# Graph layer with running maxima: three PSUM banks for the running rows, marks in two halves, table split tile by tile

## Chip, core and metric

One core of one Trainium2 chip. The metric is the device time of the kernel in microseconds; lower is better. Engines are named as in the profile: PE (TensorE), PEld (its weight loads), DVE (VectorE), ACT (ScalarE), POOL (GpSimd), SP (SyncE, which here only issues DMAs).

## What is computed

```python
# x (6250, 256) f32; src, dst (100000,) int32, sorted by dst; theta_w, phi_w (256, 256); theta_b, phi_b (256,)
x_src, x_dst = x[src], x[dst]
theta_x = (x_dst - x_src) @ theta_w.T + theta_b
phi_x = x_src @ phi_w.T + phi_b
e = jax.nn.relu(theta_x + phi_x)
out = jax.ops.segment_max(e, dst, num_segments=x.shape[0])
out = jnp.where(jnp.isfinite(out), out, 0.0)
return _layernorm(x + out, axis=-1)          # eps 1e-5
```

Since the edges are sorted by dst, the part that depends on src is b = x @ (phi - theta).T, and a node's result is relu(a + max of b over its edges), with a = x @ theta.T + biases.

## The kernel before, in words

The 100,000 edges lie as 128 partitions times 782 steps; partition p walks through its own 782 consecutive edges. At step k one row of b (256 f32) is needed for every partition, and one DVE instruction, the fold (L899), makes the running maximum: new = max(min(former, reset), row), where reset is a column with one number per partition that wipes the former value when a new node begins. The steps form 261 groups of three (GROUP). The kernel has these stages.

- **Table** (from the start to some 62 us). PE makes 49 tiles of b (L651), in seven chunks of seven; ACT copies each out of PSUM (L532). The tiles go to a table in HBM (L382, SP). At the same time each tile is split into three bf16 parts: ACT makes the first (L534) and second (L522), DVE the remainders `rest` (L832) and the third part (L824), in units of four and three tiles, so as instructions over 1024 and 768 elements. DVE's have two tensor inputs, both in SBUF. Meanwhile POOL gathers 51 x rows by indirect DMA (`early`, L464); ahead of the units DVE prepares `reset` and other columns (L785 to L818).
- **Fold loop** (to some 939 us). Most rows of b come by indirect DMA from the table, issued by POOL (L478), one per step, 679 of them, into a ring of 18 (`rows`). Before a group POOL waits until the fold that read the slot 18 gathers earlier is done (L476). The other steps, always the first of a group, get their rows in other ways: 51 from x rows that PE turns (L689) and converts (L697), with copies by ACT at L573 and L569; 40 from products of one-hot matrices (L851, DVE) with the bf16 parts in SBUF (L673, PE), in ten batches of 49, copied by ACT at L599 and L606; 12 from DMAs of one row each (L396 by SP, L562 by ACT). HOT_AT gives 2.12 one-hots to each group; six of them may be ahead of PE.
- In a group, the first two folds write `acc` in PSUM (two rows of a bank, the two banks in turn), and the third writes `hist` in SBUF, a ring of 18 rows. So the first fold of a group reads the former row from `hist`, the other two from `acc`. ACT then copies the two rows of `acc` to `hist` (L581), DVE waits for the copy of group g - 2 before it folds group g, and SP writes the group's three rows to HBM (L429, `runmax`). In the last eight groups (from LATE on) all folds write `hist`, and after each fold DVE also keeps the row at which each partition's last complete node ends (look_at, L871, `late_max`).
- **Marks.** In every fourth group DVE makes three small masks (L910 to L916), PE spreads the dst numbers of one node tile over the partitions into `ps_d` (L707, L708; two banks), and ACT, one group later, counts with one Sign activation over 782 columns how many edges lie up to a node (L588, L590). At EDGES_AT (L918) DVE makes row numbers of the counts.
- **a tiles** (in the fold loop's last part): L734 on PE, L950 on DVE.
- **End.** After the last fold: PE turns the last maxima, DVE scans over the partitions (L956), joins `late_max`, a gathered row `fix` and the carry (L961, L964), POOL scatters the result (L495) and gathers 49 tiles of maxima (L504), and DVE and ACT add, apply relu and normalise (L996 to L1016, L615).

The order on each engine is the order in the text of its loop over g, with semaphores between engines. Nothing else plans it. Behind an ACT copy in group g stand, in this order, its row loads, the Sign, and the copies of the products; ahead of it stand L569 and L573.

Of the kernel before, what the change touches and what calls it, by code (L numbers as in the profile page):

```python
# [39 lines left out]
def build(nc, x, xt, src_first, src_direct, src_act, src, src_t, dst, theta_t, phi_t, theta_b, phi_b, out):  # L40
# [6 lines left out]
    HALF = 2 * D  # L47
# [4 lines left out]
    assert HALF < STEPS <= 2 * HALF and NT * P <= 1 << 13 and 2 * CHUNK <= SLOTS  # L52
# [65 lines left out]
    LATE_STEPS = STEPS - KEPT  # L118
    assert ENDS_AT < LATE and CLEAR_AT < LATE
# [38 lines left out]
    with ExitStack() as ctx:  # L158
# [6 lines left out]
        def sem(name):  # L165
# [48 lines left out]
        in_row = sb("in_row", [P, NT])  # L214
        edges = sb("edges", [P, NT + 1])
# [43 lines left out]
        acc = ps("acc", [P, 4, D])  # L259
# [3 lines left out]
        ps_d = ps("ps_d", [P, 4, D])  # L263
        dst_rows = ps_d[:].rearrange("p j d -> p (j d)")
        rows_of_nodes = dst_rows[:, 4 * D - NT:4 * D]
        assert STEPS <= 4 * D - NT
        b_psum = [acc[:, 0, :], acc[:, 2, :], ps_t[:, 0, :], ps_a[0][:, 0, :], ps_a[1][:, 0, :], ps_a[2][:, 0, :],
                  ps_d[:, 0, :]]
# [30 lines left out]
        s_copied = sem("groups_copied")  # L299
# [50 lines left out]
        def _(sp):  # L350
# [64 lines left out]
            for g in range(NG):  # L415
# [39 lines left out]
        def _(pool):  # L455
# [15 lines left out]
            pool.wait_ge(s_rest, UNITS)  # L471
# [39 lines left out]
        def _(act):  # L511
# [6 lines left out]
            def second_part(u):  # L518
                tiles, _ = unit(u)
                n = tiles.stop - tiles.start  # L520
                act.wait_ge(s_rest, u + 1)
                nc.scalar.copy(split[:, 1, tiles, :], rest[:, u % 2, 0:n, :]).then_inc(s_split2, 1)  # L522

            for u in range(UNITS):
                c, part = divmod(u, 2)
                tiles, places = unit(u)
                if c >= 2:
                    act.wait_ge(s_bout[c % 2], 16 * (c // 2))
                    act.wait_ge(s_rest, u - 3)
# [35 lines left out]
            for g in range(NG):  # L565
# [19 lines left out]
                if g in SIGN_AT:  # L585
                    t = SIGN_AT[g]
                    act.wait_ge(s_dstrow, t + 1)
                    nc.scalar.activation(dst_rows[:, 0:STEPS], dst_rows[:, 0:STEPS], ACT.Sign, bias=part_up[:, 0:1],  # L588
                                         scale=-1.0, accum_out=in_row[:, t:t + 1]).then_inc(s_inrow, 1)
# [51 lines left out]
        def _(pe):  # L641
# [18 lines left out]
            def select(b, t):  # L660
                i = b * NT + t
                if i == 0:
                    pe.wait_ge(s_split1, UNITS)
                    pe.wait_ge(s_split2, UNITS)
                    pe.wait_ge(s_split3, UNITS)
# [16 lines left out]
            for g in range(NG):  # L682
# [69 lines left out]
        def _(dve):  # L752
# [67 lines left out]
            def third_part(u):  # L820
                tiles, _ = unit(u)
                n = tiles.stop - tiles.start
                dve.wait_ge(s_split2, u + 1)
                nc.vector.scalar_tensor_tensor(split[:, 2, tiles, :], split[:, 1, tiles, :], -1.0, rest[:, u % 2, 0:n, :],  # L824
                                               ALU.mult, ALU.add).then_inc(s_split3, 1)

            for u in range(UNITS):
                tiles, places = unit(u)
                dve.wait_ge(s_split1, u + 1)
                if u >= 2:  # L830
                    dve.wait_ge(s_split3, u - 1)
                nc.vector.scalar_tensor_tensor(rest[:, u % 2, 0:tiles.stop - tiles.start, :], split[:, 0, tiles, :], -1.0,  # L832
                                               rows[:, places, :], ALU.mult, ALU.add).then_inc(s_rest, 1)
# [10 lines left out]
            def mark_sources(b, t):  # L844
# [4 lines left out]
                elif i == 0:  # L849
                    dve.wait_ge(s_split3, UNITS)  # L850
# [15 lines left out]
            def look_at(k, row):  # L866
                i = k - KEPT
                dve.wait_ge(s_fold, k + 1)
                if i:
                    dve.wait_ge(s_late, i)  # L870
                nc.vector.scalar_tensor_tensor(late_max[:], row, is_fix[:, i:i + 1], late_max[:], ALU.min,  # L871
                                               ALU.max).then_inc(s_late, 1)

            former, before = none[:], None
            for g in range(NG):
                n, slot, at = STOP[g] - START[g], g % HELD * GROUP, g % 2 * 2
# [8 lines left out]
                if 2 <= g < LATE:  # L885
                    dve.wait_ge(s_copied, g - 1)
                for s in range(n):
# [5 lines left out]
                    new = acc[:, at + s, :] if s < n - 1 and g < LATE else hist[:, slot + s, :]  # L893
                    if s == (n - 1 if g < LATE else 0) and g >= HELD:
                        dve.wait_ge(s_hout[g % HELD], 16 * (g // HELD))
# [169 lines left out]
```

## Time and profile before

| | |
|---|---|
| median of 3 runs | 1024.68 us (1023.37 to 1027.84) |
| profiled execution | 1024.78 us, span 1022.9 us |
| PE, DVE, ACT, POOL busy | 825.9, 692.4, 338.2, 762.6 us |
| mean granted TensorE clock | 0.929 |
| folds end, scatter of the fixed rows starts | 939.4, 943.2 us |

Busy time leaves out register, branch, semaphore and DMA-issuing instructions, save POOL's indirect DMAs, where the time is that of making their descriptors. A row of a view begins with line, engine, operation, output <- inputs, shapes and count.

### The profile page before, as it was taken

Reading aid. Unit: us, or ns where it says so; the run is one execution under the profiler, and the core shown is the slowest. Engines: PE = TensorE matmul, PEld = TensorE weight load, DVE = VectorE, ACT = ScalarE, POOL = GpSimd, SP = SyncE. Lnnn points to the kernel's source line nnn. Section 1 sums busy time; section 2 is a strip of 40 time slices with the busy share of each in tenths; the row PEclk is TensorE's granted clock in tenths of the full one; section 3 lists DMA queues with packets and bytes.
Section 4 is the critical chain, followed back from the end, with each engine's and each line's share of the span. In section 5 each row is a group of like instructions: output and inputs, shape, how many; then the busy total and the mean of one; then the engine's idle time right before and its main releaser. Section 6 shows DMA issues by size and latency. Waiting matters only on the chain. (4 is left out here: it accounts for less than half of the span.)

```text
span 1022.9 us, 17761 instructions
## 1 busy us (share of the span) xinstructions
PE 825.9 (81%) x3806; PEld 436.7 (43%) x3875; DVE 692.4 (68%) x1733; ACT 338.2 (33%) x701; POOL 762.6 (75%) x788
## 2 busy tenths in 40 slices
PE   5977899999999999999999999999998846560000
PEld 5833444445454545555445455445443324340000
DVE  6645666776676767667767676767665646565798
ACT  4831233333332333242333242333231121110466
POOL 7777777777777777777777777777777777775773
PEclk9979999999999999999999999999999969985555
DMA  8955767777777777867777877777776789975465
GB/s 281 379 180 181 224 223 242 230 254 236 257 235 246 243 229 252 267 221 257 239 242 241 262 226 251 240 250 237 257 226 219 235 279 308 284 241 164 122 203 176
DMA packets 117745, 243.93 MB, mean 238 GB/s; under 512 B 20241, under 2 KB 58982, under 8 KB 117638
## 3 DMA queue, kind: packets, MB, share of 16 engines
q1 hardware_dynamic: 78244, 138.69, 37.7%
q0 software_dynamic: 37488, 102.39, 35.1%
q10 hardware_dynamic: 1906, 1.72, 0.7%
q8 instruction: 31, 0.51, 0.2%
q14 instruction: 76, 0.62, 0.2%
HBM read 127.30 MB, written 115.45 MB: 237 GB/s over the span
## 5 line engine op out<-in xcount | busy, mean ns | idle before, releaser
L478 POOL DMA_INDIRECT rows<-b_table,idx x679 | 654.6, 964 | 207.0 <-issue 173.8
L673 PE MATMUL ps_a<-work,shared 128*128 128x512 bf16 x2876 | 657.1, 381 | 36.9 <-DVE work L851 33.1
L673 PEld LDWEIGHTS ps_a<-work,shared 128*128 128x128 bf16 x2940 | 282.3, 98 | 375.5 <-DVE work L851 37.2
L581 ACT COPY hist<-acc 128x512 f32<-128x512 f32 x253 | 148.7, 588 | 362.2 <-DVE hist L899 358.3
L899 DVE SCALAR_TENSOR_TENSOR acc<-hist,reset,rows 128x256 f32<-128x256 f32 x149 | 73.5, 494 | 198.2 <-issue 151.4
L851 DVE TENSOR_SCALAR work<-batch,node 128x512 bf16<-128x512 int16 x490 | 160.5, 371 | 6.1 <-PE ps_a L673 6.1
L899 DVE SCALAR_TENSOR_TENSOR acc<-acc,reset,rows 128x256 f32<-128x256 f32 x253 | 124.7, 493 | 40.7 <-DMA rows<-b_table,idx 26.8
L899 DVE SCALAR_TENSOR_TENSOR hist<-acc,reset,rows 128x256 f32<-128x256 f32 x253 | 122.3, 483 | 26.2 <-DVE acc L899 0.5
L734 PE MATMUL ps_a<-theta_sb,shared 128*128 128x256 f32 x196 | 54.4, 429 | 39.2 <-DVE shared L950 30.6
L464 POOL DMA_INDIRECT early<-in_x,idx_first x51 | 56.2, 1103 | 17.1 <-issue 14.9
L734 PEld LDWEIGHTS ps_a<-theta_sb,shared 128*128 128x128 f32 x196 | 39.9, 213 | 53.8 <-issue 48.2
L588 ACT ACTIVATE ps_d<-ps_d,part_up 128x782 f32<-128x782 f32 x49 | 43.6, 889 | 53.3 <-issue 50.3
L504 POOL DMA_INDIRECT rows<-runmax,end_row x49 | 48.4, 987 | 16.3 <-issue 14.6
L697 PE MATMUL ps_rows<-diff_sb,conv_t 128*128 128x256 f32 x204 | 52.4, 379 | 0.1
L697 PEld LDWEIGHTS ps_rows<-diff_sb,conv_t 128*128 128x128 f32 x204 | 38.4, 190 | 9.4
L573 ACT COPY conv_t<-ps_rows 128x256 f32<-128x256 f32 x51 | 19.1, 374 | 67.1 <-PE ps_rows L689 49.4
L569 ACT COPY early<-ps_rows 128x256 f32<-128x256 f32 x51 | 19.1, 375 | 63.8 <-PE ps_rows L697 61.4
L615 ACT ACTIVATE hist<-hist,shift,rstd 128x256 f32<-128x256 f32 x49 | 25.4, 586 | 0.0
L899 DVE SCALAR_TENSOR_TENSOR acc<-hist,reset,early 128x256 f32<-128x256 f32 x51 | 24.6, 482 | 0.2 <-issue 0.2
L651 PE MATMUL acc<-diff_sb,hist 128*128 128x256 f32 x56 | 15.0, 415 | 11.3 <-DMA hist<-in_xt 11.3
L832 DVE SCALAR_TENSOR_TENSOR work<-shared,rows 128x1024 f32<-128x1024 bf16 (+1 forms) x14 | 15.2, 1090 | 12.5 <-ACT shared L534 12.5
L707 PE MATMUL ps_d<-from_tile,row_of 128*128 128x270 bf16 (+1 forms) x93 | 23.1, 326 | 0.3
(133 smaller groups left out, 483.9 us busy)
## 6 DMA issues: line engine op xcount, KB each, us to landing
runmax<-hist SPq DMA_DIRECT2D x260, 384.0 KB
direct<-b_table SPq DMA_DIRECT2D x896, 1.0 KB
rows<-b_table,idx POOLq DMA_INDIRECT x679, 3.5
b_table<-rows SPq DMA_DIRECT2D x7, 896.0 KB, 7.6
shared<-in_xt SPq DMA_DIRECT2D x49, 128.0 KB, 4.4
early<-in_x SPq DMA_DIRECT2D x12, 512.0 KB
out<-hist SPq DMA_DIRECT2D x11, 512.0 KB, 3.3
late_max<-b_table ACTq DMA_DIRECT2D x256, 1.0 KB
```

The lines of the kernel that those rows point to most:

```text
L464: pool.indirect_dma_start(out=early[:, e, :], out_offset=None, in_=x, in_offset=bass.IndirectOffsetOnAxis(ap=idx_first[:, e:e + 1], axis=0 ...
L478: pool.indirect_dma_start(out=rows[:, PLACE[k], :], out_offset=None, in_=b_table, in_offset=bass.IndirectOffsetOnAxis(ap=idx[:, k:k + 1], ...
L504: pool.indirect_dma_start(out=rows[:, slot + i, :], out_offset=None, in_=runmax, in_offset=bass.IndirectOffsetOnAxis(ap=end_row[:, t + i:t ...
L581: nc.scalar.copy(hist[:, slot:slot + n - 1, :], acc[:, at:at + n - 1, :]).then_inc(s_copied, 1)
L588: nc.scalar.activation(dst_rows[:, 0:STEPS], dst_rows[:, 0:STEPS], ACT.Sign, bias=part_up[:, 0:1], scale=-1.0, accum_out=in_row[:, t:t + 1 ...
L615: nc.scalar.activation(hist[:, i, :], hist[:, i, :], ACT.Identity, scale=rstd[:, i:i + 1], bias=shift[:, i:i + 1]).then_inc(s_norm, 1)
L673: mm = pe.matmul(ps_a[banks(b)[k]][:].rearrange("p j d -> p (j d)"), split[:, part, t, k * P:(k + 1) * P], hot[:, i % HOT, :], start=(t == ...
L697: mm = pe.matmul(ps_b[:, 0, :], conv_t[:, k, :], diff_sb[:, k, :], start=(k == 0), stop=(k == KC - 1))
L707: pe.matmul(dst_rows[:, at:at + n], row_of[:], from_tile[:, at:at + n], start=True, stop=True)
L734: mm = pe.matmul(ps_a[t % 2][:, 0, :], xt_late[:, t % (2 * CHUNK), k, :], theta_sb[:, k, :], start=(k == 0), stop=(k == KC - 1))
L851: nc.vector.tensor_scalar(hot[:, i % HOT, :], short_sources[:, b % 2, :], node[:, t:t + 1], None, ALU.is_equal).then_inc(s_hot, 1)
L899: nc.vector.scalar_tensor_tensor(new, former, reset[:, k:k + 1], row_at(k), ALU.min, ALU.max).then_inc(s_fold, 1)
```

## The change

All folds but the last four now write `acc`, which is a ring of six rows in three banks. ACT copies pairs of rows to `hist`, pair (k, k+1) when fold k + 2 is done; fold k, for even k, waits for the copy of the pair that is six steps back. Copies go on to the end of the loop. look_at reads `acc` and comes after every second fold; for the last four steps it keeps its maximum in a PSUM row (`late_acc`), joined with one more instruction at the end. `ps_d` has one bank, so a node tile's marks are spread and counted in two halves of 391 columns, two groups apart. The remainders and third parts of the table are made tile by tile.

```diff
-    HALF = 2 * D
+    HALF = STEPS // 2
...
-    SPREAD_AT = {5 + 4 * t: t for t in range(NT)}
-    SIGN_AT = {6 + 4 * t: t for t in range(NT)}
-    EDGES_AT, ENDS_AT = 4 + 4 * NT, 8 + 4 * NT
+    SPREAD_AT = {5 + 4 * t + 2 * half: (t, half) for t in range(NT) for half in range(2)}
+    SIGN_AT = {6 + 4 * t + 2 * half: (t, half) for t in range(NT) for half in range(2)}
+    EDGES_AT, ENDS_AT = 7 + 4 * NT, 11 + 4 * NT
...
+    ROUND = 6
+    COPIED = STEPS - 4
+    PAIRS_AT = [range(max(0, STOP[g - 1] - 1) // 2 if g else 0, max(0, min(STOP[g], COPIED + 1) - 1) // 2) for g in range(NG)]
...
-        acc = ps("acc", [P, 4, D])
+        acc = ps("acc", [P, ROUND, D])
...
-        ps_d = ps("ps_d", [P, 4, D])
+        ps_d = ps("ps_d", [P, 2, D])
...
-                if g < LATE:
-                    sp.wait_ge(s_copied, g + 1)
-                else:
+                sp.wait_ge(s_copied, (min(STOP[g], COPIED) + 1) // 2)
+                if STOP[g] > COPIED:
                     sp.wait_ge(s_fold, STOP[g])
...
-                if g == LATE:
-                    break
-                n, slot, at = STOP[g] - START[g], g % HELD * GROUP, g % 2 * 2
-                act.wait_ge(s_fold, STOP[g])
-                if g >= HELD:
-                    act.wait_ge(s_hout[g % HELD], 16 * (g // HELD))
-                nc.scalar.copy(hist[:, slot:slot + n - 1, :], acc[:, at:at + n - 1, :]).then_inc(s_copied, 1)
+                for pair in PAIRS_AT[g]:
+                    k = 2 * pair
+                    act.wait_ge(s_fold, k + 3)
+                    for before in written((k, k + 1)):
+                        act.wait_ge(s_hout[before % HELD], 16 * (before // HELD + 1))
+                    nc.scalar.copy(hist[:, k % SLOTS:k % SLOTS + 2, :],
+                                   acc[:, k % ROUND:k % ROUND + 2, :]).then_inc(s_copied, 1)
...
-                    nc.scalar.activation(dst_rows[:, 0:STEPS], dst_rows[:, 0:STEPS], ACT.Sign, bias=part_up[:, 0:1],
-                                         scale=-1.0, accum_out=in_row[:, t:t + 1]).then_inc(s_inrow, 1)
+                    nc.scalar.activation(dst_rows[:, 0:HALF], dst_rows[:, 0:HALF], ACT.Sign, bias=part_up[:, 0:1],
+                                         scale=-1.0, accum_out=in_half[:, half, t:t + 1]).then_inc(s_inrow, 1)
...
-                    t = SPREAD_AT[g]
-                    pe.wait_ge(s_from, t + 1)
-                    pe.wait_ge(s_rowof, t + 1)
-                    if t:
-                        pe.wait_ge(s_inrow, t)
-                    for at, n in ((0, HALF), (HALF, STEPS - HALF)):
-                        pe.matmul(dst_rows[:, at:at + n], row_of[:], from_tile[:, at:at + n], start=True, stop=True)
-                    pe.matmul(rows_of_nodes[:, t:t + 1], row_of[:], p_col[:], start=True,
+                    t, half = SPREAD_AT[g]
+                    if not half:
+                        pe.wait_ge(s_from, t + 1)
+                        pe.wait_ge(s_rowof, t + 1)
+                    if t or half:
+                        pe.wait_ge(s_inrow, 2 * t + half)
+                    if not half:
+                        pe.matmul(rows_of_nodes[:, t:t + 1], row_of[:], p_col[:], start=True, stop=True)
+                    pe.matmul(dst_rows[:, 0:HALF], row_of[:], from_tile[:, half * HALF:(half + 1) * HALF], start=True,
                               stop=True).then_inc(s_dstrow, 1)
...
-                nc.vector.scalar_tensor_tensor(split[:, 2, tiles, :], split[:, 1, tiles, :], -1.0, rest[:, u % 2, 0:n, :],
-                                               ALU.mult, ALU.add).then_inc(s_split3, 1)
+                for t in range(tiles.start, tiles.stop):
+                    nc.vector.scalar_tensor_tensor(split[:, 2, t, :], split[:, 1, t, :], -1.0,
+                                                   rest[:, u % 2, t - tiles.start, :], ALU.mult,
+                                                   ALU.add).then_inc(s_split3, 1)
...
-                if 2 <= g < LATE:
-                    dve.wait_ge(s_copied, g - 1)
...
-                    new = acc[:, at + s, :] if s < n - 1 and g < LATE else hist[:, slot + s, :]
+                    new = acc[:, k % ROUND, :] if k < COPIED else hist[:, k % SLOTS, :]
+                    if k < COPIED and k % 2 == 0 and k >= ROUND:
+                        dve.wait_ge(s_copied, (k - ROUND) // 2 + 1)
...
-                    if k > KEPT:
-                        look_at(k - 1, hist[:, before, :])
-                    before = slot + s
+                    if KEPT < k < COPIED and k % 2:
+                        for i in range(k - 1, k + 1):
+                            look_at(i, acc[:, i % ROUND, :], late_max[:], False)
+                    elif k == KEPT:
+                        look_at(k, new, late_max[:], False)
+                    elif k > COPIED:
+                        look_at(k - 1, hist[:, (k - 1) % SLOTS, :], late_acc, k - 1 == COPIED)
...
+            nc.vector.scalar_tensor_tensor(fix[:], late_acc, 1.0, fix[:], ALU.mult, ALU.max).then_inc(s_best, 1)
+            dve.wait_ge(s_best, 1)
             nc.vector.tensor_tensor(late_max[:], late_max[:], fix[:], ALU.max).then_inc(s_best, 1)
```

## Rows read from the trace of the kernel before

**Rows 1.** The page's chain that ended last, and the longest waits of the span.

```profile
DVE 4%; POOL 2%; issue 2%; DMA 1%; ACT 0%; PE 0%; POOLq 0%; DVEq 0%
...
POOL rows L478 <- issue: 173.8, 570, 0.3
...
DVE acc L899 <- ACT hist L581: 29.1, 28, 4.1
```

**Rows 2.** POOL by line, one line's instructions: duration ns min/median/max.

```profile
L464 POOL DMA_INDIRECT early<-in_x,idx_first x51: 942/946/1917, 3.8 to 74.3; - x51
...
L478 POOL DMA_INDIRECT rows<-b_table,idx x679: 942/946/2067, 75.6 to 934.8; - x170
```

**Rows 3.** POOL's groups by stretch (0:75, 75:912, 912:937): busy us, mean ns, idle.

```profile
L464 POOL DMA_INDIRECT early<-in_x,idx_first x51 | 56.2, 1103 | 17.1 <-issue 14.9 <-DMA idx_first<-in_src_first 1.9 <-DVE work L832 0.3
...
L478 POOL DMA_INDIRECT rows<-b_table,idx x661 | 635.6, 962 | 201.5 <-issue 169.8 <-DVE acc L899 22.2 <-DVE hist L899 9.4
...
L478 POOL DMA_INDIRECT rows<-b_table,idx x19 | 20.0, 1051 | 5.8 <-issue 4.3 <-DVE hist L899 0.9 <-DMA runmax<-hist 0.6
```

**Rows 4.** Timeline of POOL, then of DVE, 45 to 61 us: start us, us.

```profile
46.53 1.80 POOL L464 DMA_INDIRECT early<-in_x,idx_first  x1 [0.30 <-issue]
...
46.29 1.22 DVE L824 SCALAR_TENSOR_TENSOR shared<-shared,work 128x1024 bf16<-128x1024 bf16 x1
...
59.46 2.09 DVE L824 SCALAR_TENSOR_TENSOR shared<-shared,work 128x1024 bf16<-128x1024 bf16 x2
```

**Rows 5.** Timeline of POOL, then of DVE, 453 to 457 us.

```profile
453.69 1.11 POOL L478 DMA_INDIRECT rows<-b_table,idx  x1 [0.30 <-issue]
455.11 1.08 POOL L478 DMA_INDIRECT rows<-b_table,idx  x1 [0.30 <-DVE hist L899]
...
453.50 0.49 DVE L899 SCALAR_TENSOR_TENSOR acc<-hist,reset,rows 128x256 f32<-128x256 f32 x1 [2.25 <-ACT hist L581]
...
454.63 0.48 DVE L899 SCALAR_TENSOR_TENSOR hist<-acc,reset,rows 128x256 f32<-128x256 f32 x1
455.03 0.61 DVE L851 TENSOR_SCALAR work<-batch,node 128x512 bf16<-128x512 int16 x2
```

**Rows 6.** Timeline of all engines, 583 to 592 us.

```profile
585.11 3.37 ACTq L562 DMA_DIRECT2D late_max<-b_table  x3
...
586.71 0.48 DVE L899 SCALAR_TENSOR_TENSOR hist<-acc,reset,rows 128x256 f32<-128x256 f32 x1
586.86 0.95 POOL L478 DMA_INDIRECT rows<-b_table,idx  x1 [0.30 <-issue]
```

**Rows 7.** Timeline of the fold loop's last microseconds.

```profile
934.79 2.07 POOL L478 DMA_INDIRECT rows<-b_table,idx  x1 [0.30 <-issue]
935.56 0.48 DVE L871 SCALAR_TENSOR_TENSOR late_max<-hist,is_fix,late_max 128x256 f32<-128x256 f32 x1
...
940.95 0.40 DVE L961 TENSOR_TENSOR late_max<-late_max,fix 128x256 f32<-128x256 f32 x1
...
941.88 0.42 DVE L964 TENSOR_TENSOR late_max<-late_max,ps_rows 128x256 f32<-128x256 f32 x1 [0.53 <-PE ps_rows L747]
```

**Rows 8.** DVE's, ACT's costliest groups of the page: busy us, mean ns, idle before.

```profile
L581 ACT COPY hist<-acc 128x512 f32<-128x512 f32 x253 | 148.7, 588 | 362.2 <-DVE hist L899 358.3
L899 DVE SCALAR_TENSOR_TENSOR acc<-hist,reset,rows 128x256 f32<-128x256 f32 x149 | 73.5, 494 | 198.2 <-issue 151.4
L851 DVE TENSOR_SCALAR work<-batch,node 128x512 bf16<-128x512 int16 x490 | 160.5, 371 | 6.1 <-PE ps_a L673 6.1
...
L588 ACT ACTIVATE ps_d<-ps_d,part_up 128x782 f32<-128x782 f32 x49 | 43.6, 889 | 53.3 <-issue 50.3
```

**Rows 9.** Windows: us, then busy (x) of PE, PEld, DVE, ACT, POOL; clock.

```profile
382.00:482.00 100.00, 99.47 (x479) 50.61 (x488) 71.64 (x186) 33.55 (x70) 75.89 (x80) 1.00 0.76 249
...
682.00:782.00 100.00, 93.08 (x430) 44.65 (x437) 67.24 (x180) 28.40 (x55) 75.93 (x80) 0.98 0.74 238
782.00:832.00 50.00, 35.77 (x162) 16.07 (x163) 27.27 (x68) 9.76 (x17) 37.91 (x40) 0.91 0.72 232
```

**Rows 10.** L950, one tile of 128x256 alone.

```profile
L950 DVE SCALAR_TENSOR_TENSOR shared<-ps_a,bias x49: 408/414/425, 837.6 to 921.6; 128x256 f32<-128x256 f32 x49
```

More of the change, by code:

```diff
@@ L51, in build @@
     assert NT % CHUNK == 0 and CHUNKS % 2 == 1 and D % P == 0 and sum(PARTS) == CHUNK
-    assert HALF < STEPS <= 2 * HALF and NT * P <= 1 << 13 and 2 * CHUNK <= SLOTS
+    assert STEPS == 2 * HALF and NT * P <= 1 << 13 and 2 * CHUNK <= SLOTS
     START = list(range(0, STEPS, GROUP))
@@ L118, in build, with written @@
     LATE_STEPS = STEPS - KEPT
+    ROUND = 6
+    COPIED = STEPS - 4
+    PAIRS_AT = [range(max(0, STOP[g - 1] - 1) // 2 if g else 0, max(0, min(STOP[g], COPIED + 1) - 1) // 2) for g in range(NG)]
+    assert COPIED % 2 == 0 and PAIRS_AT[-1].stop == COPIED // 2 and SLOTS % 2 == 0
+    def written(rows):
+        return {(k - SLOTS) // GROUP for k in rows if k >= SLOTS}
     assert ENDS_AT < LATE and CLEAR_AT < LATE
@@ L214, in build @@
         in_row = sb("in_row", [P, NT])
+        in_half = sb("in_half", [P, 2, NT])
         edges = sb("edges", [P, NT + 1])
@@ L262, in build @@
         ps_a = [ps(f"ps_a{i}", [P, 2, D]) for i in range(3)]
-        ps_d = ps("ps_d", [P, 4, D])
+        ps_d = ps("ps_d", [P, 2, D])
         dst_rows = ps_d[:].rearrange("p j d -> p (j d)")
[L265 to L268, printed above, removed]
+        rows_of_nodes = dst_rows[:, 2 * D - NT:2 * D]
+        late_acc = ps_d[:, 0, :]
+        assert HALF <= 2 * D - NT
+        b_psum = [acc[:, 0, :], acc[:, 2, :], acc[:, 4, :], ps_t[:, 0, :], ps_a[0][:, 0, :], ps_a[1][:, 0, :],
+                  ps_a[2][:, 0, :]]
         assert len(b_psum) == CHUNK
@@ L470, in _ @@
             pool.wait_ge(s_bout[1], 16 * (CHUNKS // 2))
-            pool.wait_ge(s_rest, UNITS)
+            pool.wait_ge(s_rest, NT)
             for g in range(NG):
@@ L520, in second_part @@
                 n = tiles.stop - tiles.start
-                act.wait_ge(s_rest, u + 1)
+                act.wait_ge(s_rest, tiles.stop)
                 nc.scalar.copy(split[:, 1, tiles, :], rest[:, u % 2, 0:n, :]).then_inc(s_split2, 1)
@@ L830, in _ @@
                 if u >= 2:
-                    dve.wait_ge(s_split3, u - 1)
-                nc.vector.scalar_tensor_tensor(rest[:, u % 2, 0:tiles.stop - tiles.start, :], split[:, 0, tiles, :], -1.0,
-                                               rows[:, places, :], ALU.mult, ALU.add).then_inc(s_rest, 1)
+                    dve.wait_ge(s_split3, unit(u - 2)[0].stop)
+                for t in range(tiles.start, tiles.stop):
+                    i = t - tiles.start
+                    nc.vector.scalar_tensor_tensor(rest[:, u % 2, i, :], split[:, 0, t, :], -1.0,
+                                                   rows[:, places.start + i, :], ALU.mult, ALU.add).then_inc(s_rest, 1)
                 if u:
@@ L864, in row_at, with look_at @@
                 return rows[:, PLACE[k], :] if k in PLACE else early[:, EARLY_OF[k], :]
-            def look_at(k, row):
+            looked = [0]
+            def look_at(k, row, best, first):
                 i = k - KEPT
                 dve.wait_ge(s_fold, k + 1)
-                if i:
-                    dve.wait_ge(s_late, i)
-                nc.vector.scalar_tensor_tensor(late_max[:], row, is_fix[:, i:i + 1], late_max[:], ALU.min,
+                if looked[0]:
+                    dve.wait_ge(s_late, looked[0])
+                looked[0] += 1
+                nc.vector.scalar_tensor_tensor(best, row, is_fix[:, i:i + 1], late_max[:] if first else best, ALU.min,
                                                ALU.max).then_inc(s_late, 1)
-            former, before = none[:], None
+            former = none[:]
             for g in range(NG):
-                n, slot, at = STOP[g] - START[g], g % HELD * GROUP, g % 2 * 2
+                n = STOP[g] - START[g]
                 if START[g] in EARLY_OF:
@@ L892, in _ @@
                         dve.wait_ge(s_got[g % LANDED], ARRIVED[g])
-                    new = acc[:, at + s, :] if s < n - 1 and g < LATE else hist[:, slot + s, :]
-                    if s == (n - 1 if g < LATE else 0) and g >= HELD:
-                        dve.wait_ge(s_hout[g % HELD], 16 * (g // HELD))
+                    new = acc[:, k % ROUND, :] if k < COPIED else hist[:, k % SLOTS, :]
+                    if k < COPIED and k % 2 == 0 and k >= ROUND:
+                        dve.wait_ge(s_copied, (k - ROUND) // 2 + 1)
+                    if k >= COPIED:
+                        for earlier in written((k,)):
+                            dve.wait_ge(s_hout[earlier % HELD], 16 * (earlier // HELD + 1))
                     if k:
@@ L918, in _ @@
                 if g == EDGES_AT:
-                    dve.wait_ge(s_inrow, NT)
+                    dve.wait_ge(s_inrow, 2 * NT)
+                    then(nc.vector.tensor_tensor(in_row[:], in_half[:, 0, :], in_half[:, 1, :], ALU.add))
                     then(nc.vector.tensor_scalar(in_row[:], in_row[:], 0.5, 0.5 * STEPS, ALU.mult, ALU.add))
@@ L951, in _ @@
                                                    ALU.add).then_inc(s_aev, 1)
-            look_at(STEPS - 1, former)
+            look_at(STEPS - 1, former, late_acc, False)
             dve.wait_ge(s_lastt, 1)
```

17 lines of the change are left out of this document (8 added, 9 removed).

## The prediction

> **What bounds the kernel now.** First the chain of waits: it holds little more than the last tenth of the span, and its long pieces are POOL's indirect DMAs and, behind them, DVE's work on the output tiles [rows 1]. So the question is what POOL waited for earlier, and the list of waits answers it: of 679 gathers 570 stand behind "issue", never over 0.3 us at a time [rows 1]. By line [rows 2], an undisturbed gather takes 0.946 us (the median), the x rows' and the table's alike, and the gap is always 0.30. POOL therefore runs one gather each 1.25 us from 3.8 us to 937 us and waits for nobody, neither for the table nor for a free slot. DVE, with 198 us idle before the first fold of its groups, waits for POOL [rows 8]. Nothing that other engines do in that stretch counts unless it makes a gather longer, or makes POOL wait at all.
>
> Some gathers are longer. By stretch [rows 3], the 51 early ones took 56.2 us, 8.0 over 51 x 0.946; the next 661 took 635.6, 10.3 over; the last 19 took 20.0, 2.0 over. That is 20.3 us of POOL's time and nearly all that any edit to the other engines can return before 937 us.
>
> What stretches them shows when POOL's timeline is laid beside DVE's. In [rows 4] a gather begins at 46.53 and takes 1.80, 0.85 too long. A remainder instruction of DVE with two inputs in SBUF runs from 46.29 to 47.51. In [rows 5] the gather of 453.69 took 1.11, and a fold that reads `hist` and `rows` runs from 453.50 to 453.99. The sum is the same in both: the excess is the end of DVE's instruction less POOL's start less 0.135 us (0.98 - 0.135 = 0.85; 0.30 - 0.135 = 0.165), if DVE's began at least 0.08 before POOL's. The next gather in [rows 5], from 455.11, took 1.08: the first of two one-hot instructions (L851) began 0.08 before it. I went through all starts between 75.5 and 912 us in this way. Of 101 gathers that began with a fold reading `hist` under way 42 were stretched, 4.7 us in all (first at 93.09, last at 908.68), and L851 accounts for about 5.2. Of the 171 that began under a fold with its former row in PSUM none was stretched, as at 586.86 in [rows 6].
>
> **The folds in PSUM.** After the change a fold has one SBUF input. This removes the 4.7 us of the first folds, with an occasional second hold (4.9 with starts where both kinds overlap). What of L851's 5.2? Some twenty of its hits are a consequence of a fold hit: POOL, released at the fold's end, starts the next gather 0.49 - 0.135 + 1.25 = 1.605 us after the fold's start, and the first L851 starts 1.53 after it (455.03 - 453.50), always 0.08 ahead [rows 5]. These go with their cause. Against that, L851 moves: three folds through PSUM at 0.59 spacing, the distance that a fold reading the one before it in `acc` shows, end about 0.1 us later than now, and other groups come to lie badly. Without any lock, 480 L851 meet a window of 0.135 us (0.08 to 0.215 before a gather) in 1.25, with 0.067 us each: 52 x 0.067 = 3.5 us. The bounds are 0 and about 8 (each group's second L851 in the window that now holds the most first folds). I take 3.6 left of 10.3: **6.7 us saved** (2.3 to 10.3).
>
> Weighed against this is the Trainium skill, SBUF — State Buffer, Who interferes with whom. It says that a DVE instruction with two SBUF inputs contends with a GpSimd instruction that reads SBUF, the loser waiting to the end; but also that such an instruction takes only the pair's read interface, while making descriptors needs the write interface (marked as inferred). By its second half this change would return nothing and the time would stay at 1025. This trace sides with the first half: 1.80 against 0.946 with only such an instruction beside it [rows 4].
>
> **The last eight groups.** There folds and look_at both read two SBUF tensors, 46 instructions of 0.48, and the last gather took 2.07 [rows 7], through the ends of four of them in a row. After the change only the folds of steps 779 to 781 have two SBUF inputs. Of 2.0 us I take **1.8 saved** (1.0 to 2.0), the greater part of it in the last gather, whose landing releases the last fold.
>
> **The table tile by tile.** Of the 8.0 us over, 1.05 lie in the preparation ahead of the units, which stays; 6.9 come from L832 and L824, 28 instructions of 0.95 to 1.23. They become 98 of some 0.42 (a tile's instruction took 0.414 [rows 10]), and two that follow each other start about 0.33 apart. A gather that begins under one now waits at most 0.42 - 0.08 - 0.135 = 0.2 us, with a mean near 0.065, and about 26 begin under one: 1.7 us. **5.2 us saved**. Could POOL miss the gap between two instructions that overlap by 0.08, and wait out all four tiles? In [rows 4] it did not: two L824 follow each other from 59.46, and the gather of 59.70 ended with the first. The 2.07 in [rows 7] says that it can. The bounds are then 7 saved, and 1 lost (four times 0.33 plus 0.09 is 1.41 against 1.23). DVE's work grows by some 28 x 0.15 = 4 us, but it waits for ACT's casts there, and the table is in HBM by 62.6 while POOL comes to it at 75 (now 70): covered, cost 0. If that cover of 7 us were gone the loss would be one for one.
>
> **More copies, smaller slack.** 389 pair copies replace 253 at 0.588 [rows 8]: ACT has 80 us more, and 49 more Signs of half width (0.889 for 782 columns; half of them between 0.45 and 0.889, I take 0.55, plus the accumulator read of 0.19) add 49 x 0.6 = 29. ACT goes from 338 to 447 us of 1011, no bound. But in even groups the pair of rows 3g - 2 and 3g - 1 stands behind L569 or L573, which wait for PE's previous group, and is wanted by the group's fifth fold from its start; before, the seventh. PE has no idle time to hide (99.5 of 100 us busy in mid-loop [rows 9]), so DVE will wait more often for ACT: 29.1 us in 28 waits now [rows 1], I take 60 to 80. Folds in PSUM take 0.25 us more a group, 63 us. Both come out of DVE's idle time (198 us before first folds alone [rows 8]). POOL notices only when DVE is more than 18 x 1.25 - 3.5 (landing) - 4 = 15 us behind. None of it counts: **0**. SP writes a group about one group later, at 16 of the 20 us that the `hist` ring allows; 0 as well. POOL's queue is not touched.
>
> **The end.** The two last look_at go through PSUM one after the other (0.1 later), and the added join of 0.42 stands before L961 and L964. L961 ended at 941.35 and L964 began at 941.88 [rows 7], so of 0.47 about 0.53 is free: **0.2 us added** (0.1 to 0.6). From the scatter at 943.2 to the end nothing changes.
>
> **Sum.** 1024.8 (profiled execution: 1022.9 of span and 1.9 around it; the median of the runs is the same within 0.1) - 5.2 - 6.7 - 1.8 + 0.2 = **1011.3 us**. All bounds together give 1024.8 - 7 - 10.3 - 2 + 0.1 = 1005.6 and 1024.8 + 1 - 2.3 - 1 + 0.6 = 1023.1, but they would have to fall together.
>
> **Rivals.** (a) The contention moves: L851 comes to lie on POOL's starts (6 to 8 us instead of 3.6), or POOL waits out chains of tiles in the table. For it: this kernel's phases are locked, so hits are not random; against it: most chains seen let POOL in. Half of the table's gain and 3 us of the loop's are gone: 1011.3 + 2.6 + 3.2 = 1017. (b) Nothing moves: what stretched the gathers was not the second SBUF input but something that goes with it. For it only the page's sentence above; against it 0 of 171. Time 1025. (c) Slower: PE waits for the Sign. Today a tile's Sign has three groups; now each half has one. Behind the group's last fold ACT makes a copy (0.59), three row loads (1.3, but 3.37 where row numbers are loaded [rows 6]), Sign and read (0.74), 2.6 to 4.7 us, while PE has 2.12 x 6 matmuls of 100/479 us, 2.7 us, before it asks. PE's own spare time before the products end is at least 6.9 + 14.2 us [rows 9], then DVE may lag 15 us. So it decides from (21 + 15)/98 = 0.37 us for each of 98 waits; at 0.6 us it costs 59 - 36 = 23: 1034. Against it: where PE lags behind DVE, as it does in most of the loop, the Sign is done when PE comes.
>
> **How the numbers follow.** Forecast 0.74, (a) 0.13, (b) 0.05, (c) 0.08. A difference under 0.5% (5.1 us) can't be told from none. Faster: the first and nearly all of (a), 0.86; same 0.06; slower 0.08. The forecast's own bounds reach from 1006.5 to 1016; with (a) the range ends at 1019, and (b), (c) and the far ends, under 0.2, are left out.
>
> **What would show it.** Right: POOL's early group near 50 us busy for 51 (from 56.2), the 679 gathers near 646 (from 654.6), still with gaps of 0.3 only; no stretched gather under a fold; the last gather below 1.2 us. DVE's wait for ACT above 29 and without effect. Wrong: gathers stretched under folds with a PSUM input, a wait of POOL for a fold over 1 us, PE idle before the spreads (L707, L708), or a scatter that starts more than 4.5 us after the last fold.

## The result and the profile after

The changed kernel takes 1012.7 us in the median (1012.2 to 1012.9), the kernel before 1025.2: ratio 0.9875, 95% interval 0.9853 to 0.9898. The forecast was 1011.3, range 1006.5 to 1019. The profiled execution has a span of 1011.1 us, 11.8 shorter.

The page of the changed kernel, its costliest groups (busy us, mean ns, idle before):

```profile
L488 POOL DMA_INDIRECT rows<-b_table,idx x679 | 646.1, 952 | 207.0 <-issue 181.4
...
L590 ACT COPY hist<-acc 128x512 f32<-128x512 f32 x389 | 221.5, 592 | 224.9 <-DVE acc L917 222.8
...
L598 ACT ACTIVATE ps_d<-ps_d,part_up 128x391 f32<-128x391 f32 x98 | 55.3, 564 | 70.8 <-issue 67.5
L474 POOL DMA_INDIRECT early<-in_x,idx_first x51 | 52.1, 1021 | 17.2 <-issue 15.2
```

POOL's idle time is what it was, 207.0 us, in gaps of 0.3; its gathers are shorter. The same groups by stretch, POOL alone, 71 to 900 us and 900 to 925 us, answer to [rows 3]:

```profile
L488 POOL DMA_INDIRECT rows<-b_table,idx x660 | 628.2, 952 | 201.2 <-issue 176.5 <-DVE acc L917 24.7
...
L488 POOL DMA_INDIRECT rows<-b_table,idx x20 | 18.9, 946 | 6.1 <-issue 4.9 <-DVE acc L917 0.6 <-DMA runmax<-hist 0.6
```

Over 0.946 us each, the early gathers are now 3.9 us too long (8.0 before), the loop's 3.8 (10.3), the last twenty 0 (2.0). The three savings are 4.1, 6.5 and 2.0, together 12.6; the forecast had 5.2, 6.7 and 1.8.

Folds no longer stretch a gather. A start counts here when it lies at least 0.08 us after the start of the DVE instruction and more than 0.135 us before its end. Before, 42 of 48 such starts under a fold that reads `hist` were stretched by over 0.04 us, and none of 98 under a fold that reads `acc`; now all folds of the loop read `acc` and none of 161 starts was stretched. The one-hots (L865) still stretch theirs, 44 of 45 by over 0.02 us, though they have one tensor input; by what they hold POOL no run here separates.

By line (duration ns min/median/max), the longest gather of the loop fell from 2067 to 1107 ns [rows 2]:

```profile
L488 POOL DMA_INDIRECT rows<-b_table,idx x679: 942/946/1107, 71.5 to 923.4; - x170
```

In the table stage, timeline of POOL and then of DVE, 45 to 61 us, to be read against [rows 4]:

```profile
45.61 1.11 POOL L474 DMA_INDIRECT early<-in_x,idx_first  x1 [0.30 <-issue]
47.02 1.04 POOL L474 DMA_INDIRECT early<-in_x,idx_first  x1 [0.30 <-issue]
48.37 0.94 POOL L474 DMA_INDIRECT early<-in_x,idx_first  x1 [0.30 <-issue]
...
45.48 1.43 DVE L846 SCALAR_TENSOR_TENSOR work<-shared,rows 128x256 f32<-128x256 bf16 x4 [1.24 <-ACT shared L544]
46.83 1.09 DVE L835 SCALAR_TENSOR_TENSOR shared<-shared,work 128x256 bf16<-128x256 bf16 x3
```

The gather of 45.61 began under four tile instructions in a row that last until 46.91, and took 1.11. Held to 46.91 it would have taken 2.11 (1.30 - 0.135 + 0.946): POOL got in after one of them. Of 27 gathers that began under such instructions 19 were stretched, by 2.3 us in all; the other eight began within 0.02 us of the start of the next one in the row.

The end, timeline of all engines, answers to [rows 7]:

```profile
923.43 0.95 POOL L488 DMA_INDIRECT rows<-b_table,idx  x1 [0.30 <-issue]
...
926.84 0.48 DVE L917 SCALAR_TENSOR_TENSOR hist<-hist,reset,rows 128x256 f32<-128x256 f32 x1
927.23 1.07 DVE L888 SCALAR_TENSOR_TENSOR ps_d<-hist,is_fix,ps_d 128x256 f32<-128x256 f32 x2
...
928.86 0.40 DVE L984 SCALAR_TENSOR_TENSOR fix<-ps_d,fix 128x256 f32<-128x256 f32 x1
...
929.79 0.42 DVE L989 TENSOR_TENSOR late_max<-late_max,ps_rows 128x256 f32<-128x256 f32 x1
931.24 1.03 POOL L505 DMA_INDIRECT runmax<-late_max,fix_row  x1 [5.54 <-issue]
```

POOL's last gather now ends at 924.38 and not 936.86, 12.5 us earlier, the last fold starts 12.1 us earlier (926.84 for 938.92), the scatter 12.0 (931.24 for 943.21), and the end comes 11.8 earlier. The 0.4 lost between the first two is a wait that took the place of one: before, the last fold waited for its row (2.1 us behind the gather); now the row is there, and the fold follows DVE's own folds and look_at without a gap.

The engines that were thought to come under pressure (waits of the whole span):

```profile
DVE acc L917 <- ACT hist L590: 14.2, 16, 3.1
...
DVE from_tile L937 <- PE ps_d L719: 11.1, 16, 1.6
...
PE ps_d L719 <- ACT ps_d L598: 1.7, 5, 0.5
```

DVE waits for ACT's copies half as long as before (29.1 us), not longer, and PE almost never waits for a Sign (2.2 us in 6 waits with those of L718). A new wait stands ahead of the masks: DVE may not overwrite `from_tile` until PE has spread its second half. It is within DVE's idle time.

For the experiments one thing must be known: beside ten of the twelve runs the kernel before itself took 1377 to 1393 us in the median, not 1025, and POOL was not the bound. Such runs are marked **P**. In their ten traces ACT waits 298 to 551 us and DVE 160 to 260 us for what the profile calls "remote", a semaphore raised by nothing that it recorded, up to 18.7 us at a time; the four traces at 1011 to 1041 us have no such wait. The mean granted TensorE clock is 0.81 to 0.84 in them, against 0.92 to 0.93. What is cause and what consequence there is open. P times are compared only with the kernel before that was timed beside them; the length of a single gather can be read in them as elsewhere, since the median one takes 0.946 to 0.949 us there too. Only the last two, e8_sbuf_five and e6c_nine, met a kernel before at 1027 us.

### The profile page after: what moved, and what is told of

Same layout as the page of the kernel before. It is cut to its first block, busy times and chain, and to the rows that moved or that the text cites. A ratio compares the mean times of both kernels' runs of the same rounds, so it can differ in the third digit from the quotient of the medians.

```text
span 1011.1 us, 18234 instructions
## 1 busy us (share of the span) xinstructions
PE 832.0 (82%) x3875; PEld 438.2 (43%) x3875; DVE 696.6 (69%) x1805; ACT 421.4 (42%) x935; POOL 750.0 (74%) x788
## 4 chain that ended last, share of the span: by engine, by line
PE 34%; POOL 21%; DMA 18%; issue 11%; DVE 11%; ACT 2%; ACTq 2%; SPq 0%; DVEq 0%; POOLq 0%
PE ps_a L683 28%; POOL rows L488 19%; DMA rows<-b_table,idx 14%; DVE acc L917 5%; DMA b_table<-rows 2%; PE ps_rows L707 2%; POOL rows L514 2%; DVE work L865 1%; DVE shared L1024 1%; PE acc L661 1%; ACTq L569 1%; DVE shared L1021 1%; DVE stats L1038 1%; PE ps_d L719 1%; ACT hist L590 1%
## 5 line engine op out<-in xcount | busy, mean ns | idle before, releaser
L488 POOL DMA_INDIRECT rows<-b_table,idx x679 | 646.1, 952 | 207.0 <-issue 181.4
L917 DVE SCALAR_TENSOR_TENSOR acc<-acc,reset,rows 128x256 f32<-128x256 f32 x674 | 331.5, 492 | 249.7 <-DMA rows<-b_table,idx 197.6
L590 ACT COPY hist<-acc 128x512 f32<-128x512 f32 x389 | 221.5, 592 | 224.9 <-DVE acc L917 222.8
L865 DVE TENSOR_SCALAR work<-batch,node 128x512 bf16<-128x512 int16 x490 | 160.6, 371 | 5.3 <-PE ps_a L683 5.3
L598 ACT ACTIVATE ps_d<-ps_d,part_up 128x391 f32<-128x391 f32 x98 | 55.3, 564 | 70.8 <-issue 67.5
L719 PE MATMUL ps_d<-from_tile,row_of 128*128 128x391 bf16 x98 | 32.2, 329 | 1.7 <-ACT ps_d L598 1.7
L661 PE MATMUL acc<-diff_sb,hist 128*128 128x256 f32 x84 | 22.2, 420 | 12.6 <-DMA hist<-in_xt 12.6
L937 DVE TENSOR_SCALAR from_tile<-short_dst 128x782 bf16<-128x782 int16 x49 | 19.6, 401 | 12.4 <-PE ps_d L719 11.1
L846 DVE SCALAR_TENSOR_TENSOR work<-shared,rows 128x256 f32<-128x256 bf16 x49 | 18.0, 426 | 11.1 <-ACT shared L544 10.5
L917 DVE SCALAR_TENSOR_TENSOR acc<-acc,reset,early 128x256 f32<-128x256 f32 x51 | 24.6, 481 | 0.0
L661 PEld LDWEIGHTS acc<-diff_sb,hist 128*128 128x128 f32 x84 | 17.3, 210 | 16.2 <-issue 10.6
```

What stands on the lines that cost most here:

```text
L488: pool.indirect_dma_start(out=rows[:, PLACE[k], :], out_offset=None, in_=b_table, in_offset=bass.IndirectOffsetOnAxis(ap=idx[:, k:k + 1], ...
L590: nc.scalar.copy(hist[:, k % SLOTS:k % SLOTS + 2, :], acc[:, k % ROUND:k % ROUND + 2, :]).then_inc(s_copied, 1)
L598: nc.scalar.activation(dst_rows[:, 0:HALF], dst_rows[:, 0:HALF], ACT.Sign, bias=part_up[:, 0:1], scale=-1.0, accum_out=in_half[:, half, t: ...
L661: mm = pe.matmul(b_psum[j], xt_sb[:, h * CHUNK + j, k, :], diff_sb[:, k, :], start=(k == 0), stop=(k == KC - 1))
L719: pe.matmul(dst_rows[:, 0:HALF], row_of[:], from_tile[:, half * HALF:(half + 1) * HALF], start=True, stop=True).then_inc(s_dstrow, 1)
L865: nc.vector.tensor_scalar(hot[:, i % HOT, :], short_sources[:, b % 2, :], node[:, t:t + 1], None, ALU.is_equal).then_inc(s_hot, 1)
```

## The experiments

Theory P (a name that has nothing to do with the mark): POOL never waits, so a gather costs 1.25 us, and each start under a DVE instruction with two SBUF inputs, or under a one-hot, adds what is left of that instruction. The rivals are in the expectations.

**e1_table (P): only the table tile by tile.** The kernel before with

```diff
-                nc.vector.scalar_tensor_tensor(rest[:, u % 2, 0:tiles.stop - tiles.start, :], split[:, 0, tiles, :], -1.0,
-                                               rows[:, places, :], ALU.mult, ALU.add).then_inc(s_rest, 1)
+                for t in range(tiles.start, tiles.stop):
+                    ...
```

> The kernel before with only the table's remainders and third parts made tile by tile. Theory P (POOL never waits, and only stretched gathers cost time): of the 7.0 us by which the early gathers exceed 0.946 us each behind the preparation about 4.7 go, as in the changed kernel (2.3 left), the fold loop stays as it was: 1025.2 - 4.7 = 1020.5. Rival T (the table is not what counts, all of the gain is the ring's): 1025 +- 1. Rival C (POOL waits out chains of overlapping tile instructions): 1025 to 1027, with gathers of over 1.5 us between 17 and 62 us.

1387.5 us, ratio 1.020 (0.992 to 1.049): it can't be told from no change. POOL's 51 early gathers took 50.0 us, but DVE stood idle for 28.8 us of that stage, and ACT and PE for 8 to 11 us at a time, so only four gathers began under a tile instruction, and that is no measure of them either. For the time it is inconclusive. Its loop, whose folds are those of the kernel before, shows both kinds of fold in one trace: 41 of 44 starts under one that reads `hist` were stretched, by 3.6 us, and none of 105 under one that reads `acc`.

**e2_ring and e2b_ring (P): only the ring, the pair copies and the halves.** The changed kernel with

```diff
-                for t in range(tiles.start, tiles.stop):
-                    i = t - tiles.start
-                    nc.vector.scalar_tensor_tensor(rest[:, u % 2, i, :], split[:, 0, t, :], -1.0,
+                nc.vector.scalar_tensor_tensor(rest[:, u % 2, 0:tiles.stop - tiles.start, :], split[:, 0, tiles, :], -1.0,
...
```

> The changed kernel with the table again in units of four and three tiles: ring of six rows, pair copies and marks in halves alone. Theory P: 6.4 us of the loop's stretched gathers and 1.9 of the last eight groups' go, 0.2 comes at the end: 1025.2 - 8.1 = 1017.1. Rival T: all of the gain, 1012.7. If the two parts share their gain (the phases of POOL and DVE fall otherwise), the sum of both savings differs from 12.5 us by more than 2.

> The same kernel as e2_ring, again, for its time where the kernel before takes 1025 and not 1377 to 1392 us. Ring, pair copies and halves alone, the table in units of four and three tiles. Theory P: 1025.2 - 8.1 = 1017.1. Rival T (all of the gain is the ring's): 1012.7. If the kernel before again takes near 1380 us, POOL isn't the bound there, and theory P expects no gain: DVE, ACT and PE wait longer for each other, and the ring's shorter slack makes it 0 to 3% slower, as in e2_ring.

1391.1 and 1404.0 us, ratios 1.024 (1.010 to 1.038) and 1.016 (1.006 to 1.025): slower, by 1 to 2%. The first ratio goes by the two shortest of seven times of the kernel before (1349.9 and 1362.9); against the median of all seven, 1377.3, it would be 1.010. The gathers are those of the changed kernel (679 in 646.4 us, none of 165 starts under a fold stretched in e2, none of 161 in e2b), so the ring shortens them, and it returns nothing where they do not set the pace. How the gain of 12.5 splits in time was not measured at 1025, and against rival T, that all of it is the ring's, speaks only the split above, which is that of POOL's durations.

**d1_two_sbuf and d2_one_psum (P): one more DVE instruction a group.** In the changed kernel, between folds and one-hots; d1 as shown, d2 with `former` for `theta_sb[:, 0, :]` (`s_spare` is a new semaphore):

```diff
+                if g < LATE:
+                    k = STOP[g]
+                    dve.wait_ge(s_fold, k)
+                    if k % 2 == 0 and k >= ROUND:
+                        dve.wait_ge(s_copied, (k - ROUND) // 2 + 1)
+                    nc.vector.scalar_tensor_tensor(acc[:, k % ROUND, :], theta_sb[:, 0, :], 1.0, bias[:], ALU.min,
+                                                   ALU.max).then_inc(s_spare, 1)
+                    dve.wait_ge(s_spare, g + 1)
```

> The changed kernel with one more DVE instruction in each of 253 groups, between the folds and the one-hots: 128x256 f32 of two inputs in SBUF (theta_sb, bias), written to the acc slot that the next fold overwrites; its value is not used. Theory P: a hold of 0.49 us catches a start of POOL with a window of 0.27 in 1.25 us, 55 times with 0.135 us: 1012.7 + 7.4 = 1020 (1016 to 1027, since the starts are not random), and gathers stretched under it. Rival W (what stretches gathers is not the second SBUF input: a DVE instruction's write, or DVE's load as such): the same time as d2_one_psum.

> The same added instruction, but its first input is the row just folded, in PSUM, so that only bias is read from SBUF. Theory P: no gather is stretched under it; DVE is busy 253 x 0.49 = 124 us more, out of some 250 us of waiting; one-hots come about 0.5 us later against POOL, so their hits move: 1012.7 + 0 (-2 to +3). Rival W: as slow as d1_two_sbuf. Rival L (DVE's load now decides, PE starved): above 1018 in both.

1393.8 and 1393.6 us: in time no difference, and none could show, as POOL waited for folds 336 and 334 us; the 1020 and 1012.7 of the forecasts were not tested. The gathers tell them apart. Timeline of POOL and DVE, d1:

```profile
380.86 1.10 POOL L489 DMA_INDIRECT rows<-b_table,idx  x1 [0.30 <-issue]
...
380.71 0.43 DVE L934 SCALAR_TENSOR_TENSOR acc<-theta_sb,bias 128x256 f32<-128x256 f32 x1
```

and d2:

```profile
372.95 0.94 POOL L489 DMA_INDIRECT rows<-b_table,idx  x1 [2.62 <-DVE acc L918]
...
372.71 0.43 DVE L934 SCALAR_TENSOR_TENSOR acc<-acc,bias 128x256 f32<-128x256 f32 x1
```

Both instructions take 0.43 us, write the same slot and stand in the same place. Of 56 starts under d1's, counted as above, 53 were stretched by over 0.03 us, by 5.5 us together (0.28 - 0.135 = 0.145 forecast for the one shown, 1.10 - 0.946 = 0.154 measured). Of 42 under d2's none was. Rival W falls: for this instruction it is the second SBUF input, neither the write nor DVE's load.

**e3_all_sbuf (P) and e8_sbuf_five: the suspected cost made larger.** The kernel before with all folds written to SBUF and no copies by ACT, as in the diff; e8 has also `DIRECT_GROUPS = (46, 89, 130, 174, 217)` and `ROWS_A_GROUP = 3`.

```diff
-                nc.scalar.copy(hist[:, slot:slot + n - 1, :], acc[:, at:at + n - 1, :]).then_inc(s_copied, 1)
...
-                    new = acc[:, at + s, :] if s < n - 1 and g < LATE else hist[:, slot + s, :]
+                    new = hist[:, slot + s, :]
```

> The kernel before with all three folds of every group written to SBUF (hist), as its last eight groups do, and without ACT's copies out of PSUM. Theory P: all folds hold two SBUF inputs, 0.40 us apart, so in most groups one of POOL's starts falls under a fold; 253 x 0.86 x about 0.1 us is 22 us in place of 4.7: 1025.2 + 17 = 1042 (1030 to 1055), POOL's gathers longer in the mean and still no wait of POOL. Rival A (the load of ACT and the longer folds through PSUM set the time; 148 us of copies and 0.2 us a group are gone): 1015 to 1025.

> e3_all_sbuf (the kernel before, all folds written to SBUF, no copies by ACT) with e7_five's five steps of rows loaded by SP: the two edits that saved time where the kernel before takes near 1385. Theory S (the pace is set there by instructions that SP and ACT issue, each for itself): the savings add, 1385 - 28 - 47 = 1310 (1295 to 1330). Rival O (both remove the same wait): 1335 to 1365. Where the kernel before takes 1025, theory P expects it slower than before: two gathers and more stretched ones, 1035 to 1055.

e3 took 1363.3 us, ratio 0.978 (0.972 to 0.983): faster, though the gathers grew to 672.7 us. That is the side of rival A (ACT's 148 us of copies gone), but the waits for these copies and the order of the writes to HBM went with them, and which of it counted was not separated. e8 met a kernel before of 1026.6 and took 1043.4, ratio 1.0165 (1.0148 to 1.0182), inside the 1035 to 1055 of theory P; theory S and rival O were not tested, as the kernel before was not at 1385. Its gathers, by line, with POOL's only named wait still "issue" at up to 0.3 us:

```profile
L475 POOL DMA_INDIRECT rows<-b_table,idx x681 | 669.9, 984 | 207.7 <-issue 176.9
...
L461 POOL DMA_INDIRECT early<-in_x,idx_first x51 | 58.1, 1139 | 17.2 <-issue 15.2
```

Against [rows 3] and the page of the kernel before that is 15.3 + 1.9 us more busy and 0.8 more in gaps, 18.0, for 16.8 us of time (18.4 between the two profiled spans); two of the gathers are additional (2.5). Of 144 starts under a fold of the loop, counted as above, 132 were stretched by over 0.02 us, by 21.0 us (4.7 before). One of them, POOL and DVE:

```profile
338.64 1.21 POOL L475 DMA_INDIRECT rows<-b_table,idx  x1 [0.31 <-issue]
...
338.54 1.00 DVE L889 SCALAR_TENSOR_TENSOR hist<-hist,reset,rows 128x256 f32<-128x256 f32 x2
```

The rest of the first fold (0.38 - 0.135 = 0.25) went by and no more: the second, 0.08 inside the first's end, did not hold POOL. In this kernel ACT has less to do than in the kernel before (198.8 us busy for 338.2), SP issues 256 row loads less and DVE is as busy (693.2 us for 692.4), and it is the slowest of the four at 1012 to 1043: the gathers decide.

**e6_nine, e6b_nine (P) and e6c_nine: two gathers less.** The changed kernel with

```diff
-DIRECT_GROUPS = (35, 69, 98, 130, 162, 194, 226)
+DIRECT_GROUPS = (30, 54, 81, 105, 131, 157, 182, 207, 234)
-ROWS_A_GROUP = 4
+ROWS_A_GROUP = 5
```

> The changed kernel with nine steps in place of seven whose rows SP loads one by one (five rows a group in place of four), so POOL has 677 gathers in place of 679. Theory P: two gathers of 1.25 us less, 1012.7 - 2.5 = 1010.2 (1009 to 1011.5). Rival Q (SP's queue or DMA traffic is near its limit; DVE waits for direct rows or for hist): 1012.7 or more, with waits of DVE for those rows.

> The same kernel as e6_nine, again, since in that comparison the kernel before took 1391 us and not 1025, and its time can't be set beside the forecast. Nine steps in place of seven have their rows loaded one by one by SP, so POOL has two gathers less. Theory P: 1012.7 - 2 x 1.25 = 1010.2 (1009 to 1011.5) where the kernel before takes 1025. Rival Q (SP's queue is near its limit): 1012.7 or more.

> The nine-step kernel (677 gathers by POOL in place of 679) once more, now that the kernel before takes 1026 us again. Theory P: two gathers of 1.25 us less than the changed kernel, 1.2% + 0.25% = 1.45% faster than before, 1012 (1010 to 1013 with before at 1026.6), with POOL never waiting. Rival Q (SP's five rows a group come too late, or fill its queue): ratio 0.9875 or more, and waits of POOL or of DVE for those rows. If the kernel before takes near 1385 again: 7.5% slower, as twice before.

Under P it was 7.5% slower, twice (ratios 1.075 and 1.0745, intervals within 1.067 to 1.082). With a kernel before of 1027.3 it took 1012.0, ratio 0.9854 (0.9837 to 0.9870), the forecast of theory P (0.9855); but the interval overlaps with the changed kernel's, so that it beats it is not shown. Rival Q (0.9875 or more) is excluded. Its profile:

```profile
L488 POOL DMA_INDIRECT rows<-b_table,idx x677 | 645.9, 954 | 206.5 <-issue 176.0
```

Two gathers less took 0.2 us less busy time and 0.5 less idle, 0.7 in all, as the span says (1010.4 for 1011.1), where the forecast had 2.5. So the ratio agrees by luck: the kernel before was 2 us slower here. One-hots stretched their gathers by 4.3 us in place of 3.8, and the rest of the missing 1.8 lies in starts that I can't assign. Among them is the only stretched one of 173 under a fold that reads `acc`, by 0.12 us; in the nine other traces with such folds that were counted there is none. What is taken off POOL comes back in part when the phases shift.

**a0_changed and e7_five (P): the changed kernel, and one with fewer rows loaded by SP.** e7 has `DIRECT_GROUPS = (46, 89, 130, 174, 217)` and `ROWS_A_GROUP = 3` in the changed kernel.

> The changed kernel once more, as it is, as the control of the runs made so far, in which the kernel before took 1377 to 1392 us. Theory P where the kernel before takes 1025: 1012.7. Where it takes near 1385: POOL is not the bound there (it waited 320 us for folds in e1_table), so the ring and the tile-wise table return nothing, and by e2_ring and d2_one_psum I expect 1385 to 1410, 0 to 2% slower than before. Rival G (the gain is of another kind and holds in both): 1.2% faster than before.

> The changed kernel with five steps in place of seven whose rows SP loads one by one, three rows a group in place of four; POOL has two gathers more. Theory P where the kernel before takes 1025: 1012.7 + 2 x 1.25 = 1015.2. Where it takes near 1385, theory S (the issue of row loads by SP sets the pace there: e6_nine, with 256 row loads more, took 107 us more, 0.42 us a row): 256 rows fewer save up to 107 us, 1290 to 1340. Rival R (the nine-step kernel was slow for another reason, as a row needed too early): within 1% of a0_changed.

a0 took 1391.5 us, ratio 1.0135 (1.0058 to 1.0211): under P the change costs 1.4%. e7 took 1344.7, ratio 0.979 (0.973 to 0.985), 47 us below a0; theory S had the side right, and its size, up to 107, too large (1344.7 lies outside its 1290 to 1340); rival R falls. The waits show what binds there, in a0:

```profile
POOL rows L488 <- DVE acc L917: 341.7, 103, 14.6
...
DVE acc L917 <- ACT hist L590: 149.9, 49, 9.9
...
ACT hist L590 <- DMA runmax<-hist: 89.4, 41, 6.8
...
PE ps_d L718 <- ACT ps_d L598: 19.9, 11, 3.1
```

and in e1_table, whose folds and copies are those of the kernel before:

```profile
POOL rows L478 <- DVE acc L902: 225.5, 74, 14.4
...
POOL rows L478 <- DVE hist L902: 99.2, 26, 10.5
DVE hist L902 <- DMA runmax<-hist: 97.2, 42, 7.8
DVE acc L902 <- ACT hist L581: 54.0, 21, 9.1
```

POOL waited 341.7 us for folds in a0 and 324.7 in e1. Behind both stand SP's writes of `hist` to HBM (`runmax`), which must be done before a row of `hist` is written again: in e1 DVE waited 97.2 us for them and 54.0 for copies, together 151.2; in a0 DVE waited 149.9 for copies, and the copies waited 89.4 for the writes. SP issues its row loads in the same queue, and the wait grows with them:

| run (P) | row loads by SP | ACT's copies waited for the writes, us | time, us |
|---|---|---|---|
| e7_five | 640 | none listed | 1344.7 |
| a0_changed | 896 | 89.4 | 1391.5 |
| e6_nine | 1152 | 249.2 | 1498.7 |

So free rows of `hist` bind more the more SP has to issue, which fits what e6 loses and e7 gains under P; no run took the writes off SP's queue. What makes the change itself 1.4% slower there was not separated: the shorter slack of the ring, priced at nothing in the forecast, the added copies, and PE's waits for Signs (24.3 us in 14 waits in a0, none in e1) are all new in it.

## Why the prediction was right, step by step

- **POOL as the bound.** Right, and the whole gain is in its gathers: 4.1 + 6.5 + 2.0 = 12.6 us against a last gather 12.5 us earlier. e8 shows the other sign, 18.0 us more of POOL's time for 16.8 of the kernel's.
- **Which instruction holds POOL.** Right: 53 of 56 with two SBUF inputs, 0 of 42 with one (d1, d2), and no start of 161 under a fold was stretched in the changed kernel. So rival (b) falls. Of the two sentences of the Trainium skill, SBUF — State Buffer, Who interferes with whom, that the prediction weighed, the one on two SBUF inputs is borne out. By the other, that such an instruction takes only the read interface while making descriptors needs the write interface, these gathers would not be held, and they were: d1's instruction writes PSUM and stretched them. They also read their row numbers (`idx`) from SBUF, and whether POOL is held at that or at making the descriptors was not separated.
- **Folds in the loop.** 6.7 forecast, 6.5 measured. The one-hots were left with 3.6 of excess by a count of random meetings (bounds 0 and 8); 45 gathers were stretched under one, by 3.8 us. That it came so near is in part luck, since the phases are not random.
- **Last groups.** 1.8 forecast, 2.0 measured.
- **Table.** 5.2 forecast, 4.1 measured: the step that was mis-sized. The tile instructions left 2.3 us (1.7 forecast), and the preparation ahead of them 1.6, which the forecast had kept at 1.05. The largest single excess is that of the gather of 10.35 us, which began under a memset of DVE (10.26 to 10.53) and took 1.82, 0.87 too long; it had not been so before. DVE's next instruction, with two SBUF inputs (line 796, 10.45 to 11.36), began 0.10 after the gather, and 11.36 - 10.35 - 0.135 = 0.875 is the excess: POOL was held to that one's end, though the folds of e8 did not hold it so. What decides between the two is open.
- **ACT.** Its busy time, 421.4, is below the 447 forecast: the copies took 72.8 us more (80 forecast), the Signs with their reads 21.5 (29), and the page counts overlapping pieces once. That DVE would wait 60 to 80 us for it was wrong: 14.2 us. A likely reason, argued and not tried: I had counted only the later deadline, not that the copy of a pair no longer waits for the group's end. Neither figure reaches the end of the kernel at 1025.
- **The end.** 0.2 forecast, 0.5 lost by the scatter, and 0.2 more by the end. With savings of 12.6 for 13.7 that is 11.9 for the 13.5 forecast, and the span gave 11.8. The added join was free (2.95 us from last fold to the last join, 2.96 before). What came instead is DVE's own queue of folds, 0.4.
- **Rivals.** (a) did not come: no chain of tiles held POOL, and the one-hots' part did not grow. (b) falls, as said. (c) did not come where POOL is the bound: PE waited 2.2 us for Signs. Where it is not, under P, its wait did appear (24.3 us in a0), and the change was 1.4% slower.

## To carry to other kernels

When one queue runs back to back, read its instruction's median against its mean: the difference, times the count, is all that the other engines can give it, and the timeline of the suspect beside it says which instruction takes it. Here a DVE instruction with one of its two inputs in PSUM cost POOL's indirect DMAs nothing (one start of 173 in e6c apart), one with both in SBUF up to its own length. A gain of this kind holds only as long as that queue is the bound; where POOL waited 342 us for folds, the same edit was 1.4% slower.

## Not expected of the hardware

- The excess of a gather is the end of the holding instruction less POOL's start less 0.135 us, to about 0.02 us in the cases shown under a fold. The meeting also locks POOL's phase: a hit of the first fold brought a hit of the one-hot with 0.13 us behind it.
- Instructions of DVE that overlap by 0.08 us with the next do not hold POOL through: 17 of the 19 stretched starts in the table had such a successor, and none was held by it. One exception of 1.12 us in the kernel before [rows 7], and the memset and its successor above, stay unexplained.
- Under P one row load more or less on SP was worth 0.42 us (e6 against the kernel before) and 0.18 (e7 against a0), and the waits for `hist` above moved with it; in e6c, 256 loads more cost nothing. What makes P is open: the packets of the DMA queues took as long as elsewhere in the profile's sums (q1 27.8% of 1383 us is 384 us, 37.7% of 1023 is 386).
